# Spiking FFN: the stores of the finished rows in another order

## The reference

```python
rates = relu(x) * DT                       # DT = 0.001
c = cond[:, None, :] + cumsum(rates, axis=1)
spikes = (floor(c) - previous floor(c)) / DT
h = relu(spikes @ w1 + b1)                 # 512 -> 2048
out = x + (h @ w2 + b2)                    # 2048 -> 512
```

## Time and profile before

| | |
|---|---|
| median of 3 runs | 106.34 us (105.84 to 106.35) |
| profiled execution | 106.16 us, of which 104.4 us are the span of the profile |
| PE busy | 89.7 us (86%) |
| DVE busy | 64.4 us (62%) |
| POOL busy | 46.0 us (44%) |
| ACT busy | 35.1 us (34%) |
| DMA moved | 29.77 MB, mean 285 GB/s |
| q1 (SP's transfers) | 6192 packets, 25.43 MB, 62.4% of 16 engines |
| q0 (POOL's transfers) | 2672 packets, 4.22 MB, 20.8% of 16 engines |

### The profile page before, as it was taken

One profiled execution on the slowest core, in us unless ns is written; L12 is line 12 of the kernel. 1 busy time (PEld: TensorE's weight loads), 2 busy tenths in 40 slices (PEclk: granted clock), 3 DMA queues, 4 the chain that ended last, 5 costly groups with the idle time before them and its releaser, 6 DMA issues.

```text
span 104.4 us, 1036 instructions
## 1 busy us (share of the span) xinstructions
PE 89.7 (86%) x307; PEld 45.9 (44%) x307; DVE 64.4 (62%) x157; ACT 35.1 (34%) x64; POOL 46.0 (44%) x47
## 2 busy tenths in 40 slices
PE   5999999999999995999999999991009999999900
PEld 5934444444644424543354454430009984444300
DVE  2449899795499999898979998979700000050020
ACT  2876515405290009993260000062004880000000
POOL 6597000000077300175035940709988872787030
PEclk9999999999999999999999999999755999999995
DMA  2999999999999999940006999999999999978501
GB/s 75 306 381 366 424 421 410 411 408 411 406 413 406 389 381 407 407 138 8 1 3 107 189 175 399 427 395 289 427 424 427 424 371 230 207 92 112 68 13 57
DMA packets 9019, 29.77 MB, mean 285 GB/s; under 512 B 2040, under 2 KB 2168, under 8 KB 7831
## 3 DMA queue, kind: packets, MB, share of 16 engines
q1 hardware_dynamic: 6192, 25.43, 62.4%
q0 software_dynamic: 2672, 4.22, 20.8%
q10 hardware_dynamic: 146, 0.01, 0.1%
HBM read 21.58 MB, written 10.75 MB: 310 GB/s over the span
## 4 chain that ended last, share of the span: by engine, by line
PE 48%; DVE 15%; DMA 14%; POOL 13%; issue 6%; POOLq 0%; DVEq 0%
PE ps_table L871 38%; DMA out<-x_sb 14%; DVE total_two L602 8%; POOL x_sb L378 6%; POOL out L371 6%; PE ps_small L982 4%; DVE x_sb L747 2%; PE ps_turn L908 2%; PE ps_idle L887 2%; POOL out L424 1%; PE ps_idle L897 1%; DVE total L605 1%; DVE under L612 1%; DVE under L624 1%; DVE blocks_under L615 1%
## 5 line engine op out<-in xcount | busy, mean ns | idle before, releaser
L871 PE MATMUL ps_table<-w_sb 128*128 128x512 f32 x128 | 58.0, 603 | 0.0
L871 PEld LDWEIGHTS ps_table<-w_sb 128*128 128x128 f32 x128 | 23.8, 193 | 27.0 <-issue 26.2
L366 POOL DMA_INDIRECT rates<-in_x_turned,sixteen_at x8 | 8.5, 1059 | 30.4 <-DVE sixteen_at L616 28.6
L467 ACT ACTIVATE w_sb<-w_sb,b_col 128x512 f32<-128x512 f32 (+2 forms) x19 | 12.2, 640 | 17.1 <-DMA w_sb<-in_w_pairs 17.0
L602 DVE SCALAR_TENSOR_TENSOR total_two<-x_sb,total_two 128x1024 f32<-128x1024 f32 x14 | 17.2, 1229 | 1.0 <-DMA x_sb<-in_x 0.6
L371 POOL DMA_INDIRECT out<-w_sb,to_single x8 | 12.4, 1552 | 4.5 <-DMA out<-x_sb 2.3
L977 PE MATMUL ps_met<-w_sb 128*128 128x512 f32 x32 | 14.2, 596 | 0.0
L468 ACT ACTIVATE w_sb<-w_sb,minus_relu_b 128x512 f32<-128x512 f32 (+2 forms) x19 | 12.3, 649 | 0.6
L747 DVE TENSOR_TENSOR x_sb<-x_sb,ps_idle 128x2048 f32<-128x2048 f32 x5 | 11.3, 2285 | 1.2 <-ACT idle_row L494 0.7
L378 POOL TENSOR_TENSOR x_sb<-x_sb,idle_row 128x512 f32<-128x512 f32 x8 | 9.9, 1260 | 3.6 <-DVEq L785 2.5
L738 DVE TENSOR_SCALAR failed<-ps_table 128x2 f32<-128x2 f32 x1 | 0.2, 159 | 17.4 <-PE ps_table L934 17.4
(11 more groups left out here) (143 smaller groups left out, 88.1 us busy)
## 6 DMA issues: line engine op xcount, KB each, us to landing
x_sb<-in_x SPq DMA_DIRECT2D x16, 512.0 KB, 13.3
out<-x_sb SPq DMA_DIRECT2D x8, 1024.0 KB, 9.0
w_sb<-in_w_pairs SPq DMA_DIRECT2D x15, 512.0 KB, 15.3
x_sb<-idle_row POOLq DMA_DIRECT2D x1, 1024.0 KB, 8.1
w_sb<-in_w_pairs SPq DMA_DIRECT2D x2, 256.0 KB, 2.9
b_row<-in_b SPq DMA_DIRECT2D x1, 256.0 KB
rates<-in_x_turned,sixteen_at POOLq DMA_INDIRECT x8
out<-w_sb,to_single POOLq DMA_INDIRECT x8, 6.4
```

The source lines that it names most:

```text
L366: pool.indirect_dma_start(out=rates[:, col, :], out_offset=None, in_=x_sixteen, in_offset=bass.IndirectOffsetOnAxis(ap=sixteen_at[:, col:c ...
L467: chain(act.activation(weights, weights, ACT.Relu, bias=b1_col[:, m:m + 1], scale=PER_DT))
L871: last = pe.matmul(ps_table[c][:, :], table_hidden[:, m, c * P:(c + 1) * P], w2_sb[:, m, :], start=(m == 0), stop=(m == FC - 1))
```

## The change

The list in L323 has its first two entries in the other order. SP now waits for `idle_added[0][1]` and stores quarter (0,1), then waits for `idle_joined[0]` and stores quarter (0,0), the accumulated one, then stores (0,2); the other five follow as before. None of these waits has to do with the gathers.

```diff
-            for b, q in ((0, 0), (0, 1), (0, 2), (0, 3), (1, 0), (1, 1), (1, 3), (1, 2)):
+            for b, q in ((0, 1), (0, 0), (0, 2), (0, 3), (1, 0), (1, 1), (1, 3), (1, 2)):
                 store_idle(b, q)
```

## The result

The changed kernel is **slower**: 108.12 us median of 4 runs (107.5 to 108.18) against 106.09 us of the kernel before in the same comparison (105.06 to 106.35), ratio 1.0188, interval 1.014 to 1.0236. The forecast was 106.1 us, same, range 104.4 to 107.6. Two later comparisons gave 1.0094 (1.0041 to 1.0148) and 1.0039 (0.9992 to 1.0085) for the same file: the 1.9% is the highest of three figures, and the other two are under 1%.

A forecast was written before the change was run, and what follows sets the result against it. The prediction took the last gather's wait for DMA engine time, plus a fixed 26.3 us tail, as the bound. Terms 0 - 0.2 + 0 + 0 gave 105.96 us from 106.16, set to 106.1 towards the median; range 104.4 to 107.6.

The forecast's parts named there:

- a fixed tail: From the last gather's landing at 78.1 us to the end at 104.4: taken as always 26.3 us.
- main case: Whole kernel: -0.2 us, running from -0.5 to +0.7 (105.66 to 106.86 us), mostly "same"; chance 0.60.
- The early store: Quarter (0,1), issued at 56.0 us, some 6.5 earlier; takes 2.7 us of engine time that accumulation or first gathers get later.
- rival A: Early store beside the accumulation is free; last gather lands at 75.4 us, 103.5 in all, or half the gain, 104.8; chance 0.22.
- work conserved: DMA engines: the early store's 2.7 us is taken from before the later stores, so 0 on the last gather's landing.
- The hole: DMA engines from 62 to 63 us, not full: the early store fills this gap, -0.5 to -0.2 us, taken as -0.2.
- The first gathers: Batch 0's two gathers, behind the accumulation on q0: land up to 2.7 us later, at 66.4 and 67.4 us.
- Gathers 3 and 4: Batch 1's two gathers, held by POOL's L389: issued 0.7 us later, hidden by traffic until about 71 us; 0, at most +0.7.
- SP's queue: SP's stores behind the accumulation: (0,2) up to 2.0 us later with less before it, (0,3) at 68.25 and later ones unchanged; 0.
- POOL behind it: POOL's adds at 70.52 us wait for DVE, not a gather, and end at 77.90; last store and add-rows keep their places; 0.
- Rival B: Last gather falls behind one more store: +2.7 us, 108.8, or only +0.7, 106.9; chance 0.18.

The follow-up runs named there:

- 28 idle matmuls: PE runs 28 ones-by-ones 128x128 matmuls before waiting for the gathers; order of before 0.9734, 0.9858, 0.9885, changed order 0.9777, 0.9895, 0.9865 of the kernel before.
- held past the issue: Kernel before, but SP holds store (0,2) until a small clear behind gather 4 has run on the POOL engine: 0.9907.
- held, ended too early: Kernel before, but SP holds store (0,2) until POOL's sequencer signals behind gather 4's issue: 0.9959.
- late gathers: Kernel before, with POOL clearing a scratch tile (some 1.3 us) before gather 3: 0.9876; with PE kept busy too, 104.62 us against 104.63 for its control.
- late restart, short: Kernel before, with PE's first layer also waiting for a 128x192 copy on ACT after the gathers have landed: 1.004.
- late restart: Kernel before, with PE's first layer also waiting for a 128x512 copy on ACT after the gathers have landed: 1.0127.

## Why the prediction was wrong

**The step that failed** is the first: "the end is the landing of the last gather plus a fixed tail, 104.4 - 78.1 = 26.3 us". The tail measured 106.3 - 78.6 = 27.7 us. The first layer's time depends on when the clock comes back, 6.94 us in one profile and 8.21 in the other, and 7.19 in a third of the same changed kernel. The page of the kernel before had it: its clock line has 7, 5, 5 in slices 29 to 31. I read the idle time of 7.31 us as a wait and never asked at what clock the work behind it ran. A main case of +0.7 us at the most with this term is 1.3 us wider, and just holds the result (108.2 against 108.12).

**What the first layer's time goes with.** In the nine profiles without 28 idle matmuls whose clock fell in PE's wait, the stretch at the lower clock lasted either 6.8 or 10.2 us. The fall and the return are worked out here from the granted clock of stretches of 0.5 and 2 us; times in us.

| profile | PE idle | from the clock's fall to PE's restart | at the lower clock | first layer |
|---|---|---|---|---|
| held past the issue | 4.73 | 2.1 | 6.8 | 7.67 |
| held, ended too early | 7.00 | 2.9 | 6.8 | 7.25 |
| changed, third comparison | 7.28 | 3.1 | 6.8 | 7.19 |
| before | 7.31 | 3.6 | 6.8 | 6.94 |
| changed, second comparison | 7.58 | 4.0 | 6.8 | 6.73 |
| late gathers | 7.53 | 4.3 | 10.2 | 8.24 |
| changed, first comparison | 7.63 | 4.3 | 10.2 | 8.21 |
| late restart, short | 6.95 | 4.7 | 10.2 | 8.04 |
| late restart | 7.29 | 4.8 | 10.2 | 7.96 |

All restarts up to 4.0 us after the fall have the short stretch, all from 4.3 on the long one. So, by these rows, a few tenths of delay can cost 1.3 us, as theory T has it. But the fall itself came 2.3 to 4.2 us into the idleness, differently in each execution, and that moves the restart against it by more than the change does.

**The early store.** Issued at 56.0 as forecast (56.16). That it takes engine time from the accumulation and not a free place was right; rival A is out (the accumulation took 11.6 or 11.7 us in all six profiles of the changed order, 8.1 or 8.2 in those of the old one). The size was off: 2.7 us forecast for the accumulation's delay, 3.6 measured. From 60 to 65 us, 1.05 MB and 0.34 MB would be 2.7 + 1.8 = 4.5 us at the rates of the earlier trace rows, and took 5.0. The zero for "work conserved" was 0.5 us there, and at the stores' end 0.9 us (90.06 against 89.02, less the common 0.18), which lay on the add-rows path, not at the end.

**The hole**, -0.2: not gained. First packets at 57.5: they came at 60, behind packets of the accumulation issued earlier, and then in turns with them. The Trainium skill (DMA: Bandwidth & Descriptors, Queues, rings and completion order) has the engines go round the queues; from 60 to 65 us the shares of 63 and 42% look like it, while the rows of 56 to 60 do not.

**The first gathers**: forecast 66.4 and 67.4, measured 66.4 and 67.2. **Gathers 3 and 4**: 0.7 us late at issue forecast, 1.3 measured (POOL issued gather 3 0.8 us after gather 1's landing, which the forecast had at nothing), and hidden as forecast, as far as the late gathers show it (104.62 against 104.63 us). The last landing was 0.3 us later beyond the common shift, inside the case's own bounds. **SP's queue and POOL behind it**: as forecast.

**Rival B** had the sign, not the mechanism. Its condition was even met, by 0.1 us: gather 4 was issued at 68.51, behind SP's (0,3) at 68.42 by the chain of waits. The price of 2.7 us did not come. The store that does count is one issued before both gathers: holding (0,2) gave 2.75 us of earlier start.

**What stays open.** A cost of the traffic of 0.3 us (0.3%) is a possibility, not a measurement: no interval shows it, and the runs below 0.95 have the other sign. Counted from the accumulation's issue, the last gather landed after 24.1 to 24.5 us in the three profiles of the changed kernel and after 24.2 in the one of the kernel before, but also after 23.3 and 23.4 in the two late-restart profiles and 24.0 to 25.7 in the four with idle matmuls, all in the old order; one execution differs from the next by more than the change. Whether the changed order makes the clock's late return more frequent, or the four runs of the first comparison were of that kind by chance, no run decides: the changed kernel's runs below 0.95 were 4 of 4, then 8 of 12 beside 13 of 29 of the kernel before, then 3 of 12 beside 11 of 23. So of the 1.9%, the clock's part is shown for the profiled execution (1.27 of 1.85 us) and by the idle matmuls, which bring both orders to within 0.4%. That the change caused it is not shown. In the two later profiles of the changed kernel, which have the short stretch at the lower clock, the tail measured 26.4 and 26.5 us, near the 26.3 of the forecast; what the forecast lacked is the case of the long stretch. Only one of the four runs of the first comparison was profiled; the two later figures make it likely that luck added to the first one.

## What to carry to other kernels

Ahead of a sum that ends in "the rest is fixed", look at the clock line behind PE's last long wait: if PE restarts at the lower clock, some tenths of delay can be worth over a microsecond, and keeping PE busy through the wait takes most of that cost away (1.1 to 2.7% here), though not all of the spread between runs. Compare such kernels more than once and look at the granted clock of each run: four runs of one comparison said 1.9%, and 24 later ones 0.9 and 0.4%. A ready store issued early is no gain where an accumulating DMA already fills the engines. What mattered for the transfer on the critical path was how many bytes were already queued when it was issued; holding back one 1 MB store until the gathers were out brought PE's start 2.75 us forward, until the next path took over.

## What the runs showed of the hardware

- The granted clock came back 3.2 us after PE's restart in the kernel before and 5.9 us after it in the changed one, with idle times of 7.31 and 7.63 us; with 7.29 us of idleness the late-start run also had the long first layer (7.96 us). The changed kernel's three profiles have 2.8, 3.8 and 5.9 us. The Trainium skill (TensorE: Matmul & The Clock Gate, Part 1: The HAM clock gate) says that the monitor runs freely and isn't reset by the kernel, so that the point of change depends on where the first matmul falls; that the same file gives three different returns agrees with it.
- An accumulating DMA within SBUF filled all engines (109%) at 0.185 MB a us, under half of a store's 0.39; with a store beside it the pair took 5.0 us, where these rates give 4.5 (an estimate).
- A transfer issued behind others waited for them: the early store, issued at 56.16 us, had no packet before 60, and from 66 to 71 us the gathers' queue had none in the kernel before.
- The stretch at the lower TensorE clock lasted 6.8 or 10.2 us in nine profiles (the table above), the long one wherever PE restarted 4.3 us or more after the fall.
- A signal by POOL's sequencer behind two gathers had released SP by 66.6 us (its next store was issued then), 0.9 us before the second of them was issued (67.52).
